# Layer 0's cross attention of a four-layer perceiver: six context buffers, eight steps written out, scores two steps ahead, paired key rows, the last key added by VectorE

## The reference, cut to what matters

```python
    def _L0_xattn_ref(k, v, q, Wk, Wv, bv, Wq, bq, Wo, bo):
        kp = jnp.einsum('bsd,ed->bse', k, Wk)
        vp = jnp.einsum('bsd,ed->bse', v, Wv) + bv
        qp = jnp.einsum('bsd,ed->bse', q, Wq) + bq
        scale = 1.0 / jnp.sqrt(jnp.float32(kp.shape[-1]))
        scores = jnp.einsum('bqd,bkd->bqk', qp, kp) * scale
        probs = jax.nn.softmax(scores, axis=-1)
        ctx = jnp.einsum('bqk,bkd->bqd', probs, vp)
        return jnp.einsum('bqd,ed->bqe', ctx, Wo) + bo
...
    x = x + _L0_xattn_ref(ctx_1024, ctx_1024, _layernorm(x, axis=-1), ...)
    x = x + _L0_attn_ref(_layernorm(x, axis=-1), ...)
```

## Time and profile before

| | |
|---|---|
| median of 3 runs | 1323.85 us (1321.8 to 1324.77) |
| the profiled execution | 1324.02 us, span of its instructions 1322.2 us |
| PE / VectorE / ScalarE / GpSimd busy over the span | 87% / 52% / 46% / 29% |
| mean granted TensorE clock | 0.908 of full speed |
| first scores of the block, in the span | 19.96 us |
| last values of the block | 55.95 to 57.61 us |
| first instruction of the next block's product (L625) | 72.67 us |

### The profile page before, as it was taken

How to read it: one execution, slowest core, us unless ns; L and a number is a source line. 1 busy time by engine, 2 the same in 40 slices (tenths; PEclk the granted TensorE clock), 3 DMA queues, 4 the chain that set the end, 5 groups by cost and what they waited for, 6 DMA issues and landing times.

```text
span 1322.2 us, 29209 instructions
## 1 busy us (share of the span) xinstructions
PE 1150.5 (87%) x10033; PEld 843.7 (64%) x10033; DVE 691.6 (52%) x2019; ACT 612.3 (46%) x1286; POOL 380.5 (29%) x551
## 2 busy tenths in 40 slices
PE   4766998999999898899997365799999999999797
PEld 1334665688777565688874154477777767888575
DVE  2276445455555543577774243634333446777653
ACT  2153223434333543577774232434343446777653
POOL 2014300121121104255550060132140504555440
PEclk8587999999999977899998657799999999999978
DMA  9510012122222001355430201011211110111000
GB/s 287 164 64 1 24 36 65 40 52 50 60 50 55 2 2 35 110 147 154 140 104 1 37 13 42 10 51 49 60 49 60 48 52 22 33 28 41 16 3 17
DMA packets 71018, 75.22 MB, mean 57 GB/s; under 512 B 6289, under 2 KB 63713, under 8 KB 70553
## 3 DMA queue, kind: packets, MB, share of 16 engines
q1 hardware_dynamic: 67880, 66.18, 18.5%
q0 software_dynamic: 1152, 6.97, 1.5%
q10 hardware_dynamic: 1904, 0.98, 0.5%
HBM read 71.49 MB, written 0.52 MB: 54 GB/s over the span
## 4 chain that ended last, share of the span: by engine, by line
PE 78%; DVE 7%; ACT 5%; DMA 4%; issue 2%; POOL 1%; ACTq 1%; SPq 1%; DVEq 0%; POOLq 0%
PE PS L498 13%; PE PS L510 13%; PE PS L1021 9%; PE PS L728 4%; PE PS L1031 4%; PE PS L692 4%; DMA CTX<-in_ctxT 2%; PE PS L501 2%; PE PS L679 2%; PE PS L735 2%; PE PS L1004 2%; PE PS L811 2%; PE PS L1051 2%; PE PS L1011 2%; ACT AR L1182 2%
## 5 line engine op out<-in xcount | busy, mean ns | idle before, releaser
L510 PEld LDWEIGHTS PS<-WB,AR 128*128 128x128 f32 x1568 | 189.5, 192 | 43.7 <-issue 40.2
L510 PE MATMUL PS<-WB,AR 128*128 128x128 f32 x1568 | 189.7, 275 | 0.0
L1182 ACT ACTIVATE AR<-PS,WB 128x512 f32<-128x512 f32 x160 | 110.0, 688 | 154.5 <-PE PS L498 148.4
L1021 PE MATMUL PS<-AR 128*128 128x257 f32 x512 | 138.5, 393 | 2.6 <-POOL AR L2494 2.6
L1753 DVE SCALAR_TENSOR_TENSOR ACC<-PS,SM,ACC 128x128 f32<-128x128 f32 x192 | 54.1, 344 | 96.0 <-PE PS L510 95.0
L1021 PEld LDWEIGHTS PS<-AR 128*128 128x128 f32 x512 | 87.1, 190 | 22.6 <-issue 8.1
L498 PE MATMUL PS<-ZT,WB 128*128 128x512 f32 x208 | 101.2, 609 | 0.0
L1628 DVE TENSOR_TENSOR AR<-PS,AR 128x512 f32<-128x512 f32 (+2 forms) x71 | 49.8, 701 | 97.3 <-ACT AR L1182 41.0
L498 PE MATMUL PS<-XNT,WB 128*128 128x512 f32 x168 | 90.5, 646 | 10.2 <-DVE AR L1628 6.0
L1182 ACT ACTIVATE AR<-PS 128x512 f32<-128x512 f32 (+2 forms) x82 | 43.5, 531 | 107.9 <-PE PS L501 75.6
L1182 ACT ACTIVATE AR<-PS,SM 128x257 f32<-128x257 f32 x136 | 64.8, 476 | 39.8 <-DVE SM L1836 30.2
(11 more groups left out here) (293 smaller groups left out, 2218.3 us busy)
## 6 DMA issues: line engine op xcount, KB each, us to landing
WB<-in_units SPq DMA_DIRECT2D x49, 385.0 KB, 3.1
CTX<-in_fside SPq DMA_DIRECT2D x32, 514.0 KB, 3.9
CTX<-in_ctxT SPq DMA_DIRECT2D x96, 130.0 KB, 2.1
CTX<-in_ctxT SPq DMA_DIRECT2D x8, 520.0 KB, 4.7
CTX<-in_ctxN SPq DMA_DIRECT2D x16, 258.0 KB
CTX<-in_ctxN SPq DMA_DIRECT2D x32, 129.0 KB, 2.3
AR<-in_ctxN SPq DMA_DIRECT2D x32, 64.5 KB, 3.0
AR<-in_l1x_w POOLq DMA_DIRECT2D x1, 2048.0 KB, 7.8
```

The source lines that it names most:

```text
L510: m = pe.matmul(PS[:, 4 + hh, 128 * t:128 * t + 128], f_h[hh][:, c, 128 * t:128 * t + 128], WB[:, q, 2 * UNIT + 128 * c:2 * UNIT + 128 * c ...
L1021: m = pe.matmul(PS[:, 2 + g, 0:KEYS], x_qb[q][:, P * g:P * g + P], x_k[q], start=True, stop=True)
L1182: return act.activation(o, i, fn, **k)
```

## The change

- **Buffers.** Six context buffers in place of two: two in `CTX`, four in `AR` from column 7172. SP issues steps 0 to 5 without a wait, and steps 6 and 7 when the values of steps 0 and 1 have been made. Behind them it waits for weight group l0 before it loads the feed-forward units.
- **Paired rows.** Partition p holds keys 2p and 2p+1 side by side, so the rows of a step are one transfer in pieces of 1032 bytes. The turn reads the weights with a step of two to match.
- **The last key** of all batches (`l0_last`, placed in `ACC`) is fetched once by four GpSimd transfers, broadcast to the 32 tokens of each batch. VectorE adds weight x row to the result in one instruction before it divides. The turn and the products for that key are gone.
- **Order.** PE makes the scores of steps 0 and 1, then: turn s, scores s+2, values s. Scores, turned weights and results have two PSUM banks each, the exponentials four buffers, and the score products read the queries where they lie. ScalarE, not VectorE, copies the turned weights out.
- **Front and tail in halves.** The query and key products are split in halves of 512 tokens between ScalarE and VectorE. In the tail the first half is turned in step 5, multiplied by `l0x_v` in step 7 before that step's values, and projected while the second half is still on its way.
- **GpSimd.** It first fetches only the row `l0x_bo` and the last keys, then adds `l0x_bo` to the stream, then waits until the rows of step 6 have landed, and only then issues the weight groups, the other 24 rows, the masks and the relative biases.
- The loops of the block are written out.

The diff, cut to its core:

```diff
-        l0_cT = [CTX[:, q, 0:4 * KPAD].rearrange("p (j k) -> p j k", j=4) for q in range(2)]
-        l0_cn = [CTX[:, q, 1040:1040 + 8 * FQ].rearrange("p (j c f) -> p j c f", j=4, c=2) for q in range(2)]
+        l0_size = 4 * KPAD + 8 * FQ
+        l0_at = lambda s: CTX[:, s % 6, 0:l0_size] if s % 6 < 2 else ar(7172 + l0_size * (s % 6 - 2), l0_size)
...
+        l0_last = ACC
...
+            def l0_load(s):
+                if s >= 6:
+                    sp.wait_ge(sig["l0s_u"], s - 5)
+                src = ctxT[4 * s:4 * s + 4, :, :].rearrange("j p k -> p j k")
+                sp.dma_start(l0_cT[s], src).then_inc(sig[f"l0_keys_landed{s % 6}"], 16)
+                src = ctxN[4 * s:4 * s + 4, 0:2 * P, :].rearrange("j (p c) f -> p j (c f)", c=2)
+                sp.dma_start(l0_cn[s].rearrange("p j c f -> p j (c f)"), src)                    .then_inc(sig[f"l0_rows_landed{s % 6}"], 16)
+            for s in range(L0X_STEPS):
+                l0_load(s)
+            sp.wait_ge(sig["w_l0"], 16)
             load_units("l0f")
...
+            l0_scores(0)
+            l0_scores(1)
+            for s in range(L0X_STEPS):
+                l0_turn(s)
+                if s + 2 < L0X_STEPS:
+                    l0_scores(s + 2)
+                if s == 1:
+                    pe.wait_ge(sig["lin_taken_d"], seen.up("lin_taken_d"))
+                if s == 7:
+                    l0_value_weights(0)
+                l0_values(s)
+                if s == 5:
+                    l0_turn_values(0)
             pe.wait_ge(sig["bias_ready"], 1)
+            carry_half(0, X)
+            l0_turn_values(1)
+            l0_project(0)
+            l0_value_weights(1)
+            carry_half(1, X)
+            l0_project(1)
...
+            def l0_turned(s):
+                act.wait_ge(sig["l0s_pt"], s + 1)
+                if s >= 2:
+                    act.wait_ge(sig["l0s_u"], s - 1)
+                act.copy(l0_pt[s % 2], PS[:, 2 + s % 2, 0:256].rearrange("p (c n) -> p c n", c=2))\
+                    .then_inc(sig["l0s_pt_taken"], 1)
...
+            l0_max(1)
+            dve.wait_ge(sig["relb_landed"], 64)
+            for s in range(L0X_STEPS):
+                l0_divide(s)
+                if s + 2 < L0X_STEPS:
+                    l0_max(s + 2)
+                l0_values(s)
...
+            for j in range(4):
+                src = ctxN[:, 2 * P:KEYS, 0:P].rearrange("(s j) o f -> j (o s) f", j=4)[j:j + 1]
+                pool.dma_start(l0_last[32 * j:32 * j + 32], src.broadcast_to([32, L0X_STEPS, P]))\
+                    .then_inc(sig["relb_landed"], 16)
...
+            normed(1)
+            pool.wait_ge(sig["rows_landed"], 16)
+            bias("l0x_bo")
+
+            pool.wait_ge(sig["l0_rows_landed0"], 32)
+            pool.wait_ge(sig["relb_landed"], 64)
             for g in ("l0", "l1", "l2", "l3"):
```

More of the change, by code:

```diff
@@ L607, in _ @@
-            l0_turn(1)
-            l0_values(L0X_STEPS - 1, 1)
-            pe.wait_ge(sig["l0s_u_taken"], seen.up("l0s_u_taken"))
-            turn(l0_u.rearrange("p (t n) -> p t n", t=NT), None)
-            pe.wait_ge(sig["bias_ready"], 1)
-            carry(X)
-            wide(4, w("l0x_v"), l0_ut, True).then_inc(sig["lin_ready"], 1)
-            pe.wait_ge(sig["lin_taken"], seen.up("lin_taken"))
-            project(l0_ct, w("l0x_o"))
+            for hh in range(2):
+                half_taken(hh)
+                pe.matmul(bank(2 + hh), w("l0x_q"), XNT[:, 512 * hh:512 * hh + 512], start=True, stop=True)\
+                    .then_inc(sig["lin_ready"], 1)
@@ new lines, in l0_turn_values, with l0_value_weights @@
+            def l0_turn_values(hh):
+                pe.wait_ge(sig["l0s_u_taken"], 4 * hh + 4)
+                for t in range(4):
+                    m = pe.transpose(PS[:, 6 - 6 * hh, P * t:P * t + P], l0_u[:, 4 * hh + t, :], ident)
+                m.then_inc(sig["turned"], 1)
+            def l0_value_weights(hh):
+                half_taken(0)
+                pe.matmul(bank(7 - 6 * hh), w("l0x_v"), l0_ut[:, 512 * hh:512 * hh + 512], start=True, stop=True)\
+                    .then_inc(sig["lin_ready"], 1)
@@ new lines, in l0_project, with carry_half @@
+            def l0_project(hh):
+                pe.wait_ge(sig["lin_taken_d"], seen.up("lin_taken_d"))
+                for t in range(4 * hh, 4 * hh + 4):
+                    m = pe.matmul(PS[:, 6 + hh, P * (t % 4):P * (t % 4) + P], l0_ct[:, P * t:P * t + P], w("l0x_o"),
+                                  start=False, stop=True, skip_group_check=True)
+                m.then_inc(sig["proj_ready"], 1)
+            def carry_half(hh, src):
+                pe.matmul(bank(6 + hh), ident, flat(src)[:, 512 * hh:512 * hh + 512], start=True, stop=False,
+                          skip_group_check=True)
@@ new lines, in _ @@
+            l0_max(0)
+            dve.wait_ge(sig["lin_ready"], 4)
+            dve.tensor_scalar(l0_qp[:, 512:1024], PS[:, 5, :], float(P) ** -0.5, None, ALU.mult)\
+                .then_inc(sig["lin_taken_d"], 1)
+            dve.wait_ge(sig["lin_taken_d"], seen.up("lin_taken_d"))
+            l0_max(1)
+            dve.wait_ge(sig["relb_landed"], 64)
+            for s in range(L0X_STEPS):
+                l0_divide(s)
+                if s + 2 < L0X_STEPS:
+                    l0_max(s + 2)
+                l0_values(s)
@@ L2441, in y_last_values @@
                 pool.wait_ge(sig["yl_ready"], seen.up("yl_ready"))
-            for k in range(2):
-                seen.up(f"ctx_landed{k}", 16 * (L0X_STEPS // 2))
             for k in range(4):
```

228 lines of the change are left out of this document (107 added, 121 removed).

## The result

The changed kernel takes 1309.69 us (median of 7 runs, 1304.78 to 1315.15), the kernel before in the same session 1323.31 (7 runs). The ratio is 0.9896 [0.9878, 0.9915]: 13.6 us faster, where 24.2 were forecast, and outside the range. The profiled execution took 1310.24 us, its span is 1308.2.

The account below looks back on a forecast made before the run. Bound by wrong bytes going first, then load latency in a ring of two, then a half-clock tail. 23.5 us gained up to the projection plus 0.7 in the norm make 24.2: 1324.02 to 1299.8 us, range 1293 to 1307.5.

Parts of the forecast that it names:

- What bounds the kernel: In the first block: wrong bytes going first, then load latency in a ring of two, then a tail at half clock.
- Front: Up to the first scores: halves shared with VectorE and less early traffic bring them at 16.4 us, before 19.96.
- The data: Context loads: 1.06 MB a step at 331 GB/s, so the rows of step 7 land at 32.5 us.
- last keys: I take nothing: Four GpSimd transfers of 1024 pieces: VectorE waits at 19 us, they land by 8 or 20; cost taken as nothing.
- the fixed time: Context loads: of 2.1 us from issue to landing of a 130 KB transfer, 1.7 us are fixed.
- The steps: Context loop: 2.4 us a step at half clock; last values end at 37.0 us, before 57.61, gain 20.6.
- either slow engines or slow data: End of last values: 39.6 us all at 1.2 GHz, or 33.6 at 2.4 GHz behind the data; 37.0 taken.
- The tail: Last values to last projection: 7.5 us, between half and full clock; projection ends at 44.5, before 68.02.
- The norm: Projection to the next block's first product, 4.65 us before: first half's statistics overlap, 0.7 us gained.
- Weights moved back: GpSimd issues the weights at 29.3 us; they land at 39, needed at about 48, costing nothing.
- rival of late weights: Group l0 and the vector rows land at 53.3 us, 5 late, giving 1305 us; chance 7%.
- Behind the block: Later blocks: nothing depends on absolute time, so what the first block wins should reach the end.

Follow-up runs that it names:

- weights early: Changed kernel, but GpSimd issues the weight groups without waiting for step 6's rows: 1318.08 us, ratio 0.9952.
- three buffers: Changed kernel, but SP issues a step's loads only when the values of three steps earlier have been made: 1332.32 us, ratio 1.0068.
- the version without the transfers: Changed kernel with the last keys spread by eight TensorE products in place of four broadcast transfers: 1308.61 us, ratio 0.989; with 49 transposes in front, 0.984 and 0.9807.
- holding the padded kernels 5.9 us: Six VectorE clears before SP's and GpSimd's first transfers: changed kernel with 65 transposes 0.984 to 0.9894; with 49 and keys spread by TensorE 0.9807 to 0.9864.
- the list put back: Small transposes ahead of TensorE's first work return its later instructions to their place in the kernel before; 65 of them on the changed kernel: ratio 0.984.
- padded: Changed kernel with 65 small transposes ahead of TensorE's first work: 1303.12 us, ratio 0.984.
- half padded: Changed kernel with 33 small transposes ahead of TensorE's first work: 1309.95 us, ratio 0.9883.
- before with 63 transposes: Kernel before with 63 small transposes in front, moving its later TensorE code to its place in the changed kernel: 1325.78 us, ratio 1.0014.
- the padded version with TensorE spreading the keys: Changed kernel with eight TensorE products in place of the four last-key transfers, and 49 transposes in front: 1303.36 and 1299.33 us, ratios 0.984 and 0.9807.

## Why the prediction was wrong, point by point

*What bounds the kernel.* Right on both counts that could be tried: wrong bytes first (weights early gives back 7 to 9 us of the 14 to 16 won) and a ring too shallow (three buffers cost all of it).

*Front.* 17.11 where 16.4 was said; the query product ended at 15.14, not 14.90. These 0.7 us are no part of the error, since from step 4 on TensorE waited for keys.

*The data: the first step that failed.* "The best long stretch ran at 331 GB/s" was applied from the first byte on. The keys of step 7 were due at 30.9 (rows at 32.5, less 1.6) and came at 34.3. Beside a line of 331 GB/s from the first issue at 0.7, three stretches differ. By 4 us 0.51 MB had moved, not 1.09: 1.8 us missing. From 4 to 12 us the rate was 223, so 1.79 MB moved in place of 2.65: 2.6 us. From 12 to 32 it was 352: 1.3 us back. That makes 3.1 of the 3.4 us.

The 2.6 us go back to the step "last keys: I take nothing". I asked only whether VectorE would wait for them. It did not: they landed 6 to 8 us after their issue. What they cost was the DMA engines' time, and so the context's. Without them, and without their 0.52 MB, step 7's scores start at 31.2, 32.0 and 30.6 in three profiles, close to the forecast's 30.9 (without their bytes the same sum gives 29.3). There other things hold as well: in the first SP issues these keys only at 24.6, when the values of step 1 are done. The 223 itself is measured, and that it goes with these transfers is shown; why pieces of 512 bytes, broadcast by the software queue, slow the other queue as well is not.

The 1.8 us are the fixed time. The sum has it once, 1.7 us, and the trace at both ends. Up to 2 us hardly a byte moves (8 GB/s), and the keys of step 7, which by the sum's own sizes end 9.44 MB into the stream, land at 34.28, though the engines had moved that much by 32.3. No run tests this term.

The Trainium skill's "DMA: Bandwidth & Descriptors" (Bandwidth, Where 436 GB/s comes from) puts the limit from HBM at about 358 GB/s a core. The context's 352 lies just under it, so 331 was not the ceiling that I took it for. But it is no ceiling of this core either: from 42 to 48 us the same trace moved 387 GB/s of weights.

*The steps.* The 2.4 us at half clock did not apply: up to 32 us the clock was full and the data set the pace at 3.0 to 3.5. From 24 to 32 TensorE was busy for 4.2 of 8 us, waiting for keys between the steps; then the clock fell to half and stayed there up to 42.3. Last values ended at 42.66 in place of 37.0. Of these 5.7 us the late keys explain 3.4. The other 2.3 are the end chain at half clock: 8.3 us from the scores of step 7 to the last values, where the forecast leaves 6.1 (30.9 to 37.0). How much of it is the clock alone shows in the second profile of the same kernel. There step 7's keys came at 34.0, but the clock was low from 24 to 27.4 and from some 34 to 37.5, and full for the last two groups of values; these ended at 40.5 and the next block started at 50.5, 2.2 us earlier. At full clock throughout, in the version without the transfers, the chain takes 5.5 us (30.56 to 36.03). The two limits were taken as "either slow engines or slow data"; they came one after the other.

*The tail.* Last values to last projection took 5.8 us (42.66 to 48.44), forecast 7.5, since the clock came back at 42.3. The norm took 4.25 (48.44 to 52.69), forecast 3.95. Together they gave 1.4 us back. So the block: 20.0 in place of 24.2, the sum of -5.7, +1.7 and -0.3.

*Weights moved back.* Issued at 33.39, 4 us later than said (the rows of step 6 were late too), and without cost, as forecast: no rival of late weights showed. The Trainium skill's "SBUF — State Buffer" (SBUF: two separate sides, the box on DMAs issued from GpSimd, and Who interferes with whom) says that VectorE's copies and scalings can keep GpSimd from writing descriptors; no wait for the weights that would bear it out as a cost shows in this trace, and GpSimd's issues of them took 6.0 us in all beside VectorE's work, 6.3 before.

*Behind the block: the second step that failed.* "Behind it nothing depends on absolute time... what is won here should reach the end." The first half stands: holding the padded kernels 5.9 us cost 6 to 8. What was overlooked is that the rest itself is changed, since the change lengthens TensorE's list and moves all its later instructions. The rest grew from 1249.5 to 1255.5 us. With the list put back, the changed kernel gains 21.2 us by its ratio (0.016 x 1323.3), where its block gained 21.9. In all, four measurements with the list put back (and nothing held) gave 0.9807 to 0.9863; the changed kernel and its versions that were not put back gave 0.9882 or more. Against it: the move cost the kernel before only 0.14%, with a rest of 1248.9 us in its profile, and one kernel differs by 0.33% between sessions. So the place of the code costs something, and 4.7 us is not a firm number for it.

The profiles show two parts of these 6 us. The stops of the kind "issue" behind the block add up to 7.5 and 7.6 us before, 9.2 and 8.5 changed, 7.3 padded, 8.3 half padded, 8.4 in before with 63 transposes. That is 1 to 2 us, and this part is shown to go with the place. The other is the clock. Added up over short stretches, the time at half clock in the rest was 205 and 201 us before, 215 in both profiles of the changed kernel, 206 padded; 10 us at half clock put off up to 5 us of work. But it was also 220 half padded, and 212 and 225 in the padded version with TensorE spreading the keys, which is not slower. Whether the place of the code acts on the clock, or the clock falls as it happens to, stays open.

With both put right, the transfers gone and the list at its old place, the change gains 21 to 25.5 us: the 24.2 of the forecast lie in between.

*Not tried:* the paired rows, the halves and the last key on VectorE each by itself.

## What to carry to other kernels

Cost a transfer by the engine time that its pieces take from the others, not only by whether somebody waits for it: four small broadcasts at the start halved what SP's queue moved for 8 us. Count loads in flight as buffers less the steps that the scores run ahead, and check the order of the list before making a ring smaller. And when a change moves a long list of instructions, compare the stretches far behind it as well; a few harmless instructions in front move its stops, and the kind "instruction" in the DMA view tells what they wait for. One profile of a kernel is not enough for such a stretch.

## What the runs showed of the hardware

- TensorE stops inside long runs of small products, 0.4 to 2.0 us each. Moving its instructions by some 130 places, at nearly the same work, moved these stops by 64 records, and the total by 4.7 us between two sessions.
- Each of 30 such stops in five profiles ended 2.2 to 2.8 us after a 0.02 MB transfer of the kind "instruction" on q8 had started.
- 0.59 MB on the software queue, most of it broadcast from pieces of 512 bytes, took 43% of all DMA engines' time for 8 us, and the mean rate was 223 GB/s, where it was 320 without the last keys. Pure context traffic, in pieces of 1032 and 1040 bytes, ran at 352; weights later ran at 387.
- The software queue, issued behind the hardware queue's loads of step 3, took twice its bytes (4.13 and 2.07 MB from 14 to 30 us).
- One and the same kernel gave 0.984 [0.9827, 0.9854] and 0.9807 [0.9793, 0.982] in two sessions: the interval of one session does not cover the next.
